# States of a gated graph network turned by VectorE's 32x32 squares and DMA, with GpSimd making the low half of the nodes

## What is computed

```python
x = LN(x + softmax_like(tanh(x q (x k)^T / ..)) * adj @ x @ v)       # attention
h = x                                                                 # gated, 5 steps:
  m = adj @ h
  z = sigmoid([m, m] @ w3.T + h @ u3.T + b);  r = sigmoid([m, m] @ w4.T + h @ u3.T + b)
  c = tanh([m, m] @ w5.T + (r * h) @ u5.T + b);  h = (1 - z) * h + z * c
x = LN(x + h)
x = LN(x + sum over 3 powers of adj of (adj^k @ x) @ W_k)             # graph convolution
x = LN(x + relu([adj_sq^T @ relu(x @ psi), x] @ phi1 + b) @ phi2 + b) # messages
```

## Time and profile before

| | |
|---|---|
| median of 3 runs | 1362.16 us (1362.12 to 1363.35) |
| profiled execution | 1361.57 us, its span 1359.8 us |
| busy, share of the span | PE 98%, PEld 87%, DVE 80%, ACT 70%, POOL 63% |
| granted TensorE clock, mean | 0.994 |
| DMA | 61.25 MB, mean 45 GB/s |

### The profile page before, as it was taken

The page is one execution under the profiler, slowest core; times in us unless marked ns, Lnnn a source line. Parts: engine busy times, 40 slices in busy tenths (PEclk is TensorE's granted clock), DMA queues, the critical chain, the costliest instruction groups (busy, mean ns, idle before and its releaser), DMA issues.

```text
span 1359.8 us, 27644 instructions
## 1 busy us (share of the span) xinstructions
PE 1328.3 (98%) x8638; PEld 1187.0 (87%) x8638; DVE 1084.3 (80%) x2546; ACT 956.1 (70%) x1727; POOL 862.6 (63%) x907
## 2 busy tenths in 40 slices
PE   8999989999999999999999999999899999999997
PEld 7999978888888888888888888887689999999996
DVE  4788878777778777787777887778688888888886
ACT  5788877777777777777777777776546666666664
POOL 5988886666666666666666666666335555555554
PEclk9999999999999999999999999999999999999999
DMA  3333332000020000120000110000212222222211
GB/s 107 93 96 106 97 116 63 1 0 0 23 86 17 0 0 0 39 85 0 0 0 0 55 40 1 0 0 17 70 55 71 71 69 69 69 69 69 69 39 40
DMA packets 60048, 61.25 MB, mean 45 GB/s; under 512 B 4690, under 2 KB 39380, under 8 KB 59988
## 3 DMA queue, kind: packets, MB, share of 16 engines
q1 hardware_dynamic: 59556, 60.31, 14.0%
q10 hardware_dynamic: 432, 0.20, 0.1%
HBM read 35.33 MB, written 25.17 MB: 44 GB/s over the span
## 4 chain that ended last, share of the span: by engine, by line
PE 91%; DVE 3%; ACT 2%; POOL 2%; issue 1%; DVEq 0%; POOLq 0%; ACTq 0%
PE psum L1111 6%; PE psum L752 5%; PE psum L754 5%; PE psum L731 5%; PE psum L379 3%; PE psum L1123 3%; PE psum L1125 3%; PE psum L795 3%; PE psum L784 3%; PE psum L797 3%; PE psum L796 3%; PE psum L767 3%; PE psum L786 3%; PE psum L789 3%; PE psum L772 3%; PE psum L771 3%
## 5 line engine op out<-in xcount | busy, mean ns | idle before, releaser
L706 POOL TENSOR_TENSOR rh_lo<-rh,rh_hi 128x512 fp32r<-128x512 f32 x160 | 206.8, 1293 | 250.9 <-ACT rh_hi L830 250.9
L712 POOL TENSOR_TENSOR h_lo<-h,h_hi 128x512 fp32r<-128x512 f32 x160 | 216.5, 1353 | 12.8
L830 ACT CAST rh_hi<-rh 128x512 fp32r<-128x512 f32 x160 | 99.4, 621 | 140.6 <-DVE rh L862 140.6
L843 DVE TENSOR_TENSOR psum<-psum,h 128x512 f32<-128x512 f32 x160 | 111.9, 700 | 102.9 <-ACT psum L834 102.9
L752 PE MATMUL psum<-adj_t_hi,hn_hi 128*128 128x256 f32 x640 | 164.2, 291 | 1.0 <-DVE m_lo L856 1.0
L754 PE MATMUL psum<-adj_t_hi,hn_lo 128*128 128x256 f32 x640 | 156.6, 280 | 0.0
L827 ACT ACTIVATE psum<-psum,bias_cols 128x512 f32<-128x512 f32 x160 | 106.6, 666 | 60.5 <-PE psum L772 58.7
L862 DVE TENSOR_TENSOR rh<-psum,h 128x512 f32<-128x512 f32 x160 | 110.1, 688 | 45.6 <-ACT psum L827 45.4
L752 PEld LDWEIGHTS psum<-adj_t_hi,hn_hi 128*128 128x128 f32 x640 | 121.0, 189 | 4.9 <-issue 1.8
L754 PEld LDWEIGHTS psum<-adj_t_hi,hn_lo 128*128 128x128 f32 x640 | 120.9, 189 | 3.0
L817 ACT ACTIVATE z<-psum,bias_cols 128x512 f32<-128x512 f32 x160 | 111.6, 698 | 0.0
(11 more groups left out here) (273 smaller groups left out, 4300.3 us busy)
## 6 DMA issues: line engine op xcount, KB each, us to landing
x_in<-in_x_dram SPq DMA_DIRECT2D x32, 256.0 KB, 3.0
x_dram<-x SPq DMA_DIRECT2D x32, 256.0 KB, 2.1
g_x<-x_dram SPq DMA_DIRECT2D x32, 256.0 KB, 3.3
h_dram<-h SPq DMA_DIRECT2D x32, 256.0 KB, 2.0
ht<-h_dram SPq DMA_DIRECT2D x32, 256.0 KB, 2.9
c_x<-x_dram SPq DMA_DIRECT2D x32, 256.0 KB, 3.0
out_dram<-res SPq DMA_DIRECT2D x32, 256.0 KB, 2.4
conv_in<-in_L_gnn_weight_dram SPq DMA_DIRECT2D x1, 448.0 KB, 5.2
```

The source lines that it names most:

```text
L706: pool.tensor_tensor(rh_lo[:, q, :], rh[:, q, :], rh_hi[:, q, :].bitcast(F32), ALU.subtract).then_inc(rh_lo_done, 1)
L712: pool.tensor_tensor(h_lo[:, q, :], h[:, (g - 1) % G, :], h_hi[:, q, :].bitcast(F32), ALU.subtract).then_inc(h_lo_done, 1)
L843: dve.tensor_tensor(cb, cb, hg, ALU.subtract).then_inc(dif_done, 1)
```

## The change

- Gated stage: no turns on TensorE. One slot after a state is made, VectorE transposes it in 32x32 squares into `squares` (`turn_squares`); four DMAs per slot put the squares on other partitions, in DRAM (`store`, runs of 512 bytes); a slot later one DMA brings the group back as `hn` (`fetch`), with nodes on partitions. A product's columns come in another order, which `tile` and `batch` undo.
- GpSimd makes hn_lo, last in its slot; ScalarE casts h_hi for every second group, ahead of z.
- Attention stage: VectorE makes the squares of x1 too, at the start of its next slot, ahead of p_lo; four more DMAs store them as `x1t_dram`, from where h is loaded in a set's first step. The ring of e is cut from 4 to 2.
- Graph stage: ht arrives with nodes on partitions; GpSimd adds it to x1 (`residual`), for group s+1 in slot s, ahead of the wait for var. The turn on TensorE and the sum on VectorE go.

```diff
-    U, R = 8, 4
+    U, R, E = 8, 4, 2
...
+                sp.wait_ge(squares_done, n + 1)
+                states = x1t_dram[bass.ds(n, 1), :, :].rearrange("o (a j) (w x) -> (o w) j a x", a=QUARTERS, w=QUARTERS)
+                for w in range(QUARTERS):
+                    sp.dma_start(states[w, :, :, :],
+                                 squares[32 * w:32 * w + 32, q, :].rearrange("j (a x) -> j a x", a=QUARTERS))\
+                      .then_inc(x1_out[q], 16)
...
+            if live(it, u, LAG_STORE):
+                n, q = s - LAG_STORE, (u - LAG_STORE) % 2
+                dve.wait_ge(x1_done, n + 1)
+                dve.wait_ge(x1_half_done, n + 1)
+                if not isinstance(it, int):
+                    dve.wait_ge(x1_out[q], it * (STORED * U // 2) + STORED * ((u - LAG_STORE) // 2))
+                elif n >= 2:
+                    dve.wait_ge(x1_out[q], STORED * (n // 2))
+                dve.transpose(squares[:, q, :].rearrange("p (a t i) -> p t a i", a=QUARTERS, t=TILES),
+                              x1[:, q, :, :].rearrange("p t (a j) -> p t a j", a=QUARTERS)).then_inc(squares_done, 1)
...
+        def load_state(g, k):
+            sp.dma_start(h[:, g, :], x1t_dram[bass.ds(k * G + g, 1), :, :].rearrange("o p c -> (o p) c"))\
+              .then_inc(x1_loaded[g], 16)
+
+        def store(base, g, k):
+
+            sp.wait_ge(squares_done, base + g + 1)
+            nodes = h_dram[k * G + g, :, :].rearrange("(q i) (a x) -> a i q x", q=QUARTERS, a=QUARTERS)
+            for a in range(QUARTERS):
+                sp.dma_start(nodes[a, :, :, :],
+                             squares[32 * a:32 * a + 32, g % 2, :].rearrange("i (q x) -> i q x", q=QUARTERS))\
+                  .then_inc(h_out[g], 16)
+
+        def fetch(base, g, k):
+
+
+            sp.wait_ge(h_out[g], stored(base))
+            sp.dma_start(hn[:, g % R, :], h_dram[k * G + g, :, :]).then_inc(hn_loaded[g % R], 16)
+
+        def move(base, g, k, started):
+            store(base, g, k)
+            if g > 0:
+                fetch(base, g - 1, k)
+            elif started:
+                fetch(base - G, G - 1, k)
...
+        for k in range(SETS):
+            base, final = k * SET_SLOTS, k * SET_SLOTS + SET_SLOTS - G
             for g in range(G):
-                sp.wait_ge(hn_lo_done, k * SET_SLOTS + (g + 1 - SET_SLOTS))
-                load(g, k)
+                move(base, g, k, False)
+            if k + 1 < SETS:
+                for g in range(G):
+                    sp.wait_ge(hn_lo_done, base + g + 1)
+                    load(g, k + 1)
+            with sp.Fori(base + G, final - G, G) as step:
+                for g in range(G):
+                    move(step, g, k, True)
             for g in range(G):
-                store(g, k - 1)
-        yield SLOTS - G - 2
+                if k == SETS - 1:
+                    yield SLOTS - G + g - 3
+                move(final - G, g, k, True)
+            if k + 1 < SETS:
+                for g in range(G):
+                    store(final, g, k)
+                    if g == 0:
+                        fetch(final - G, G - 1, k)
+                    load_state(g, k + 1)
...
-                pool.tensor_copy(h_hi[:, q, :], h[:, (g - 1) % G, :]).then_inc(h_hi_done, 1)
-                pool.wait_ge(h_hi_done, s)
+                if q:
+                    pool.tensor_copy(h_hi[:, q, :], h[:, (g - 1) % G, :]).then_inc(h_hi_done[1], 2)
+                pool.wait_ge(h_hi_done[q], hi_count(base, g))
                 pool.tensor_tensor(h_lo[:, q, :], h[:, (g - 1) % G, :], h_hi[:, q, :].bitcast(F32),
                                    ALU.subtract).then_inc(h_lo_done, 1)
+            if live(base, g, 0):
+                pool.wait_ge(hn_hi_done, s + 1)
+                src = x1[:, g, :, :].rearrange("p t (a j) -> p t a j", a=QUARTERS) if first(at) else by_tile(hn[:, g % R, :])
+                pool.tensor_tensor(hn_lo[:, g % 2, :, :].rearrange("p t (a j) -> p t a j", a=QUARTERS), src,
+                                   hn_hi[:, g % 2, :, :].rearrange("p t (a j) -> p t a j", a=QUARTERS).bitcast(F32),
+                                   ALU.subtract).then_inc(hn_lo_done, 1)
...
-        def turn(base, g, k, bank):
...
-        def slot(base, g, k):
-            s = base + g
-            if not paired(base, g):
-                if live(base, g, 0):
-                    turn(base, g, k, B_HN)
-            elif g % 2 == 0:
-                turn(base, g, k, B_HN)
-                turn(base, g + 1, k, B_HN_ODD)
...
-                act.wait_ge(hn_mm, s + 1)
+                if first(at):
+                    act.wait_ge(x1_loaded[g], k * 32 + 32)
+                else:
+                    act.wait_ge(hn_loaded[g % R], moved(at, g, k))
                 wait_count(act, m_mm, s - 1)
-                if k is not None:
-                    if not (isinstance(k, int) and k == 0):
-                        act.wait_ge(h_out[g], k * 16)
-                    act.copy(h[:, g, :], psum[:, hn_bank(base, g), :])
-                    act.copy(hn_hi[:, g % 2, :, :], x1[:, g, :, :]).then_inc(hn_hi_done, 1)
-                else:
-                    act.copy(hn_hi[:, g % 2, :, :].rearrange("p i d -> p (i d)"), psum[:, hn_bank(base, g), :]).then_inc(hn_hi_done, 1)
+                src = x1[:, g, :, :].rearrange("p t (a j) -> p t a j", a=QUARTERS) if first(at) else by_tile(hn[:, g % R, :])
+                act.copy(hn_hi[:, g % 2, :, :].rearrange("p t (a j) -> p t a j", a=QUARTERS), src).then_inc(hn_hi_done, 1)
+            if live(base, g, 1) and (g - 1) % 2 == 0:
+                if first(at):
+                    act.wait_ge(x1_loaded[g - 1], k * 32 + 32)
+                wait_count(act, r_mm, s - 2)
+                act.copy(h_hi[:, 0, :], h[:, g - 1, :]).then_inc(h_hi_done[0], 2)
...
+        def turn_squares(base, g):
+
+            s, left = base + g - 5, (g - 5) % G
+            dve.wait_ge(h_done, s + 1)
+
+            if not isinstance(s, int) or s >= 2:
+                dve.wait_ge(h_out[(left - 2) % G], stored(base if g == 7 else base - G))
+            dve.transpose(squares[:, left % 2, :], h[:, left, :]).then_inc(squares_done, 1)
+
+        def slot(base, g, k, at):
             s = base + g
             hg, cb = h[:, (g - 4) % G, :], psum[:, B_CAND[(g - 4) % 2], :]
             if live(base, g, 4):
                 dve.wait_ge(c_done, s - 3)
                 dve.tensor_tensor(cb, cb, hg, ALU.subtract).then_inc(dif_done, 1)
-            if live(base, g, 0):
-                dve.wait_ge(hn_hi_done, s + 1)
-                src = x1[:, g, :, :].rearrange("p i d -> p (i d)") if k is not None else psum[:, hn_bank(base, g), :]
-                dve.tensor_tensor(hn_lo[:, g % 2, :, :].rearrange("p i d -> p (i d)"), src,
-                                  hn_hi[:, g % 2, :, :].rearrange("p i d -> p (i d)").bitcast(F32),
-                                  ALU.subtract).then_inc(hn_lo_done, 1)
+            if live(base, g, 5):
+                turn_squares(base, g)
...
+        def residual(it, u):
+
+            s, q = it * U + u, u % 2
+            pool.wait_ge(y1_loaded[q], it * (32 * U // 2) + 32 * (u // 2 + 1))
+            wait_count(pool, x2_done, s - 1)
+            pool.tensor_tensor(y1[:, q, :, :].rearrange("p i (a j) -> p i a j", a=4),
+                               ht[:, q, :].rearrange("p (a i j) -> p i a j", a=4, i=TILES),
+                               x1[:, q, :, :].rearrange("p i (a j) -> p i a j", a=4), ALU.add).then_inc(y1_done, 1)
...
                 pool.wait_ge(x3t_hi_done, n + 1)
                 pool.tensor_tensor(x3t_lo[:, :], x3t[:, :], x3t_hi[:, :].bitcast(F32), ALU.subtract).then_inc(x3t_lo_done, 1)
+            if isinstance(it, int) and s == 0:
+                residual(0, 0)
+
+            if live(it, u, -1):
+                residual(it + (u + 1) // U, (u + 1) % U)
             pool.wait_ge(var_done, s + 1)
...
-        with eng.Fori(PEELED, GROUPS // U) as it:
+        with eng.Fori(PEELED, GROUPS // U - written_out) as it:
...
-            if live(it, u, 0):
-
-                pe.wait_ge(y1_loaded[u % 2], it * (32 * U // 2) + 32 * (u // 2 + 1))
-                wait_count(pe, y1_done, s)
-                if isinstance(it, int) and s == 0:
-                    pe.wait_ge(earlier["hn_lo_done"], earlier["pairs_end"])
-                if isinstance(it, int) and s == 2:
-                    pe.wait_ge(x2t_lo_done, 1)
-                for b in range(GB):
-                    for c in range(KC):
-                        mm = pe.transpose(psum[:, B_T1, cols(tile(b, c))], ht[:, u % 2, cols(b * KC + c)], ident[:, :])
-                mm.then_inc(y1_mm, 1)
             if live(it, u, L_W):
...
-                dve.wait_ge(y1_mm, s + 1)
-                wait_count(dve, x2_done, s - 1)
-                dve.tensor_tensor(y1[:, u % 2, :, :].rearrange("p (c b) d -> p c b d", c=KC),
-                                  psum[:, B_T1, :].rearrange("p (c b d) -> p c b d", c=KC, b=GB),
```

(46 more changed lines are left out.)

118 lines of the change are left out of this document (64 added, 54 removed).

## The result

The changed kernel takes 1479.1 us (median; 1474.9 to 1483.5), the kernel before beside it 1362.1: a ratio of 1.086, 95% interval 1.082 to 1.089. It is slower by 117 us, where 1420 was forecast with a range to 1465. The profiled execution spans 1476.5 us, with a mean granted clock of 0.972.

A forecast was written before the change was run, and what follows sets the result against it. TensorE, busy nearly throughout, was taken as the bound unless a longer loop of waits closes. 1361.6 + 10 (attention) - 21 (gated) + 71 (graph) = 1421.6, less some 2 for dropped copies, taken as 1420 us; range 1385 to 1465.

The forecast's parts named there:

- the three rings: Closed loops of waits in the attention, gated and graph stages, forecast at +10, -21 and +74 us.
- Graph ring, +74: Graph stage: loop from res through store, load and GpSimd's sum, 14.37 us a slot against 11.41; +74 us over 25 slots.
- rival 4: Graph stage: TensorE's clock falls in its waits, adding up to 0.9 us a slot, +22, to 1442 us; chance 0.12.
- Slots outside the ring, -3: Graph stage: the 7 slots other than the 25 slowed ones gain 0.4 us each, -3 us.
- The -0.4: Graph stage: each of 7 slots gets 0.4 us shorter because TensorE no longer makes four turns.
- Attention ring, +10: Attention: x_in issued behind four stores closes a two-slot loop of 11.35 us against 10.48; +10 us over 24 slots.
- Gated ring, -21: Gated stage: two-slot loop through GpSimd's hn_lo sets 4.67 us a slot; 0.13 gained in each of 160, -21 us.
- rival 3: T slow or colliding with GpSimd, 32-wide forms costlier: gated +16, attention +16, about 1463 us; chance 0.12.
- Rival 2: Gated stage: the loop of waits is hidden, TensorE runs at 4.37 us a slot, -69 for -21, 1372 us; chance 0.06.
- Overlaps of stages, 0: Where attention and gated stages overlap and in the last gated slots: no separate cost was forecast, 0 us.

## Why the prediction was wrong

The sign and the three rings were right; the size was off by 59 us and outside the range. By its steps:

- **Graph ring, +74: right.** It was 75 at full clock; taking away either half of its cause (load or place of the sum) brought back 11.33.
- **Clock, rival 4: right as a mechanism, wrong as an alternative.** It had a chance of 0.12 beside the forecast. But it sits on top of the ring and follows from it: 12 us, where 22 stood for a fall in every slot. It fell in 11 of 25 slots, and such a slot took about 1.1 us more, not 0.9.
- **Slots outside the ring, -3: this step failed, by 22 us.** I counted the slots up to the first res as 0.4 shorter each, from TensorE's work alone. What I didn't follow there was SyncE's queue: the loads of the first groups stand behind state stores that are new in this change and wait for the last gated groups (12 of them, 20.14 us). The order is written in the weave's list of slots: the run with the load ahead, which also moves two entries of that list, took 10.0 of it back, and three entries of the list another 8.7, after which the entry took 60.7 for the 59.9 of before. The -0.4 itself was too good as well: steady slots gained 0.09, as a wait for c_lo came up behind.
- **Attention ring, +10: the mechanism was right, the term mis-sized.** The shown ring was 11.82 for 11.35: T starts 0.3 late and x_in is issued 0.2 late. Rings with slower stores (five) or a later landing (three) took up to 13.4, and one load more than counted stands behind stores. It cost 20.7, within its own bounds of 6 to 27. With x_in ahead 18.0 of the 18.9 lost from the turn of slot 7 on came back.
- **Gated ring, -21: right, at -17.6** for 148 slots. Two small errors offset here: the slot is 4.71 for 4.67, but the slots before were 714.7 / 148 = 4.83 on average, not 4.80. hn_lo took 1.29 and T 0.70, without a collision, so rival 3 is out. Rival 2 took 4.37 for what is left when the ring goes; the runs gave 4.52.
- **Overlaps of stages, 0:** they cost 5.7 at the gated start and 2.7 at its end. At the start the versions take 40.7 to 45.3 us for the same stretch; no run settles these two.

The sum again with measured terms: 20.7 + 5.7 - 17.6 + 2.7 + 18.6 + 74.7 + 12 - 0.1 = 116.7. The range ended at 1465 because each slow case was set alone beside the forecast; attention in the upper half of its bounds and the clock came together, and the entry, which stood in no case, came on top.

## What to carry over

Where an instruction is put ahead of a wait in a queue written out by hand, follow each queue it touches back to whoever issues what it waits for: here nearly all the loss lay in loads issued behind stores. Moving loads gave back 101.5, 13.5 and 5.6 us, about the whole 117 (no run has these moves alone); GpSimd's order in the gated slot gave 28.5 more, and together they turned 8.6% slower into 2.5% faster. Follow it at the seams of stages as well, where queues carry the work of two. And sum up the costs that follow from each other (a new wait, and the clock that falls in it) in place of setting them side by side as rivals.
